# Selective-scan states written into three SBUF buffers by VectorE and multiplied by C in place, in a fused embedding, state-space and expert kernel

## The reference

```python
h = tok(x, ...)                        # (64, 128, 256): convolution and projection
h = h + attn(layernorm(h), ...)        # state-space block, below
h = h + ffn(layernorm(h), ...)         # top 2 of 8 experts, weighted sum

# attn, 512 inner channels d, 16 states n, scan over t (128 steps here; 64 sequences)
xc    = silu(causal_conv(x_inner))
delta = softplus(delta_raw * w_dt + b_dt)
h[t]  = exp(delta[t] * A) * h[t-1] + delta[t] * B[t] * xc[t]      # per d and n
y[t]  = sum_n h[t] * C[t]
out   = ((y + xc * D) * silu(z)) @ W_out
```

## Time and profile before

| | us |
|---|---|
| median of 3 runs (2647.75 to 2649.83) | 2648.08 |
| the profiled execution, its own time | 2650.71 |
| its span | 2648.9 |
| VectorE busy in the span | 2025.5 (76%) |
| GpSimd busy | 1929.2 (73%) |
| TensorE busy (modelled ends) | 2469.8 (93%) |
| ScalarE busy | 1559.3 (59%) |

### The profile page before, as it was taken

How to read it: one execution, slowest core, us unless ns; L and a number is a source line. 1 busy time by engine, 2 the same in 40 slices (tenths; PEclk the granted TensorE clock), 3 DMA queues, 4 the chain that set the end, 5 groups by cost and what they waited for, 6 DMA issues and landing times. The chain is left out here.

```text
span 2648.9 us, 35497 instructions
## 1 busy us (share of the span) xinstructions
PE 2469.8 (93%) x10678; PEld 1511.3 (57%) x10679; DVE 2025.5 (76%) x2052; ACT 1559.3 (59%) x3388; POOL 1929.2 (73%) x823
## 2 busy tenths in 40 slices
PE   4899999999999999999999999987599999999998
PEld 2334444444444444444444444433599999999998
DVE  1699999999999999999999999999333333333333
ACT  2677777777777777777777777764222222222222
POOL 2698999999999999999999999998322222222222
PEclk9999999999999999999999999999699999999999
DMA  2331414324143141431414314132532223222322
GB/s 44 141 116 43 157 39 154 116 59 158 38 154 117 58 158 38 154 120 55 158 38 154 122 53 156 39 141 88 189 47 48 46 46 48 46 47 46 47 47 33
DMA packets 124947, 235.85 MB, mean 89 GB/s; under 512 B 46031, under 2 KB 93170, under 8 KB 108460
## 3 DMA queue, kind: packets, MB, share of 16 engines
q1 hardware_dynamic: 96384, 199.06, 22.3%
q0 software_dynamic: 26272, 34.44, 7.7%
q10 hardware_dynamic: 2188, 1.15, 0.2%
HBM read 181.83 MB, written 53.65 MB: 89 GB/s over the span
## 5 line engine op out<-in xcount | busy, mean ns | idle before, releaser
L561 POOL TENSOR_TENSOR arena<-u,arena 128x2048 f32<-128x2048 f32 x255 | 1156.4, 4535 | 44.9 <-DVE psum L1180 41.2
L1180 DVE TENSOR_TENSOR_SCAN psum<-psum,arena 128x1024 f32<-128x1024 f32 x416 | 951.1, 2286 | 64.2 <-POOL arena L557 51.8
L1642 PE MATMUL psum<-hc,ident 128*128 128x512 f32 x1664 | 800.1, 605 | 95.0 <-DVE hc L1214 94.9
L891 ACT ACTIVATE psum<-delta,a_neg 128x508 f32<-128x508 f32 x1024 | 654.5, 670 | 0.0
L652 POOL DMA_INDIRECT out_dram<-hres,tok_id x135 | 210.6, 1560 | 548.1 <-ACT hres L1107 371.5
L1642 PEld LDWEIGHTS psum<-hc,ident 128*128 128x128 f32 x1664 | 298.1, 190 | 491.5 <-issue 290.7
L1214 DVE TENSOR_TENSOR hc<-psum,arena 128x1024 f32<-128x1024 f32 x416 | 507.8, 1221 | 9.9 <-PE psum L1642 0.9
L1481 DVE TENSOR_TENSOR z<-psum,xn 128x512 f32<-128x512 f32 x135 | 93.3, 691 | 432.6 <-issue 320.4
L1107 ACT ACTIVATE hres<-psum,tok_w 128x256 f32<-128x256 f32 x135 | 64.1, 475 | 400.4 <-PE psum L1817 382.6
L885 ACT ACTIVATE psum<-zeros 128x8 f32<-128x8 f32 x512 | 89.5, 175 | 303.4 <-DVE hc L1214 258.0
L1804 PE MATMUL psum<-xnt,yz 128*128 128x128 f32 x2160 | 264.9, 276 | 0.0
(11 more groups left out here) (219 smaller groups left out, 2840.5 us busy)
## 6 DMA issues: line engine op xcount, KB each, us to landing
arena<-ssm_rows SPq DMA_DIRECT2D x128, 1024.0 KB, 5.8
delta<-expert_rows SPq DMA_DIRECT2D x135, 129.0 KB, 2.0
h_saved_rows<-hnew SPq DMA_DIRECT2D x16, 512.0 KB, 6.8
hres<-h_saved_rows SPq DMA_DIRECT2D x16, 512.0 KB, 3.5
out_dram<-h SPq DMA_DIRECT2D x16, 512.0 KB, 2.9
arena<-in_L_ffn_wg_dram SPq DMA_DIRECT2D x8, 512.0 KB, 10.2
arena<-in_L_ffn_wi_dram SPq DMA_DIRECT2D x8, 512.0 KB, 10.8
arena<-in_L_ffn_wo_dram SPq DMA_DIRECT2D x8, 512.0 KB, 10.8
```

The costliest lines, as they stand in the source:

```text
L561: pool.tensor_tensor(dBx[k % 2], rep, b_rep[:, q * QN:(q + 1) * QN, :], ALU.mult).then_inc(dbx_ready, 1)
L891: last = nc.scalar.activation(o, d, ACT.Exp, scale=a_neg[:, c, n:n + 1])
L1180: nc.vector.tensor_tensor_scan(out_, h, src, 0.0, ALU.mult, ALU.add).then_inc(scan_done, 1)
L1642: last = nc.tensor.matmul(yacc[c % 2], ident[:, :], state[:, i, :], start=False, stop=(nth_sum[k] == LAST_SUM[c] and i == 1))
```

## The change

1. The scans of the 26 half units write into one of **three** buffers `hc` in SBUF; `exps` no longer finds its bank overwritten. The wait for the sum moves from the product to the scan (`sum_before`, three products back).
2. The product is taken in place in `hc`: both inputs, the state and `c_rep`, are then in SBUF.
3. As nothing overwrites dA's zero columns, they are written twice in all, at the start of group 0. `exps` waits for the scan two half units before, not for its product.
4. ScalarE's order: silu of z at k = 4 (10 before), one evacuation of `xnt` from 5 to 4 and one of `xi` from 10 to 11, the softplus pieces 2 and 3 at k = 1 and 10 (both at 4).
5. Room for the third buffer: `ones_row`, the first `pad_row`, `jlim`, `tile_no` and `tab` share the space of other tiles. Two `iota` go from the start to GpSimd's tail, `pad_row` is written again by VectorE in the tail, and in group 0 the scan k = 23 waits for the DMA that reads the first `pad_row`.

```diff
-        hc = [sb(f"hc{i}", [P, 2, GT]) for i in range(2)]
+        NHC = 3
+        hc = [sb(f"hc{i}", [P, 2, GT]) for i in range(NHC)]
...
+        def state_of(g, k):
+            return ON_POOL[k] if k in ON_POOL else flat(hc[(NOWN * g + nth_own[k]) % NHC][:, :, :])
+
+        def sum_before(g, k):
+            before, n = divmod(NOWN * g + nth_own[k] - NHC, NOWN)
+            return HU * before + nth_sum[OWN[n]] + 1
...
             def exps(g, k):
-                if k >= 2 and k - 2 in ON_POOL:
-                    actq.wait_ge(scan_done, HU * g + k - 1)
-                elif k >= 2:
-                    actq.wait_ge(hc_ready, NOWN * g + nth_own[k - 2] + 1)
-                else:
-                    ahead(actq, hc_ready, NOWN * (g - 1) + nth_own[HU + k - 2] + 1)
+                ahead(actq, scan_done, HU * g + k - 1)
                 dst = dA[k % 2]
-                nc.scalar.activation(dst.rearrange("p i (b t) -> p (i b) t", b=GB)[:, :, 0:1],
-                                     zeros[:, :].rearrange("p (b a) -> p b a", a=1), ACT.Copy)
+                if g == 0 and k < 2:
+                    nc.scalar.activation(dst.rearrange("p i (b t) -> p (i b) t", b=GB)[:, :, 0:1],
+                                         zeros[:, :].rearrange("p (b a) -> p b a", a=1), ACT.Copy)
...
-                    if k == 10:
+                    if k == 4:
                         silu_z(g)
                         if not last:
-                            evac_xi(g + 1, 1)
+                            evac_xnt(g + 1, 0)
                         load_exp_and_ln()
                     if not first:
-                        if k == 4:
-                            softplus_relu(g, 2)
-                            softplus_relu(g, 3)
+                        if k in (1, 10):
+                            softplus_relu(g, 2 if k == 1 else 3)
...
                 if k in ON_POOL:
                     state_free(g, k)
-                    out_ = ON_POOL[k]
                 else:
-                    out_ = h
-                nc.vector.tensor_tensor_scan(out_, h, src, 0.0, ALU.mult, ALU.add).then_inc(scan_done, 1)
+                    ahead(dve, sum_done, sum_before(g, k))
+                nc.vector.tensor_tensor_scan(state_of(g, k), flat(dA[k % 2]), src, 0.0, ALU.mult, ALU.add).then_inc(scan_done, 1)
...
-                if n >= 2:
-                    dve.wait_ge(sum_done, HU * g + nth_sum[OWN[n - 2]] + 1)
-                else:
-                    ahead(dve, sum_done, HU * (g - 1) + nth_sum[OWN[NOWN + n - 2]] + 1)
-                nc.vector.tensor_tensor(flat(hc[n % 2][:, :, :]), flat(dA[k % 2]), flat(c_rep[:, 2 * j:2 * j + 2, :]),
-                                        ALU.mult).then_inc(hc_ready, 1)
+                nc.vector.tensor_tensor(h, h, flat(c_rep[:, 2 * j:2 * j + 2, :]), ALU.mult).then_inc(hc_ready, 1)
```

More of the change, by code:

```diff
@@ L119, in audio_tower @@
         xt = [hres[0:KX, 2 * m:2 * m + 2, :].rearrange("p b c -> p (b c)") for m in range(2)]
+        ones_row = h2[0:1, 0, 0:P]
+        pad_first = h2[:, 2:4, :].rearrange("p b c -> p (b c)")[:, 0:ROW]
         row = sb("row", [P, GB, ROW])
@@ L148, in audio_tower @@
         ebase = sb("ebase", [P, E])
-        jlim = sb("jlim", [1, TOKENS // P])
-        tile_no = sb("tile_no", [1, NT])
+        NJL = TOKENS // P
+        jlim = draw[0:1, 0:NJL]
+        tile_no = draw[0:1, NJL:NJL + NT]
+        pad_row = draw[:, GT - ROW:GT]
+        assert NJL + NT <= GT - ROW
         cmp1 = z[0:1, 0, 0:E * (TOKENS // P)].rearrange("p (e j) -> p e j", e=E)
@@ L157, in audio_tower @@
         e_of, t_of, r_of, b_of = (hnew[0:1, i, 0:NT] for i in range(4))
-        tab = sb("tab", [1, 2, NT + 4], I32)
+        tab = xw[0:1, :, :, :].rearrange("p b k x -> p (b k x)")[:, 0:2 * (NT + 4)].bitcast(I32)\
+            .rearrange("p (k i) -> p k i", k=2)
         pad_at = sb("pad_at", [1, E], I32)
-        pad_row = sb("pad_row", [P, ROW])
         XB = 4
@@ L168, in audio_tower @@
         yt = [hres[:, i, :] for i in range(2)]
-        tok_id = [sb(f"tok_id{i}", [P, 1], U32) for i in range(XB)]
-        tok_w = [sb(f"tok_w{i}", [P, 1]) for i in range(XB)]
+        tok_ids, tok_ws = sb("tok_ids", [P, XB], U32), sb("tok_ws", [P, XB])
+        tok_id = [tok_ids[:, i:i + 1] for i in range(XB)]
+        tok_w = [tok_ws[:, i:i + 1] for i in range(XB)]
         psum = ctx.enter_context(nc.psum_tensor("psum", [P, 8, 512], F32))
@@ L187, in audio_tower @@
         LAST_SUM = [max(nth_sum[k] for k in range(HC * c, HC * c + HC)) for c in range(NCH)]
-        assert len(SUMS) == HU and NOWN % 2 == 0 and not ON_POOL.keys() & {0, 1, HU - 2, HU - 1}
+        assert len(SUMS) == HU and not ON_POOL.keys() & {0, 1, HU - 2, HU - 1}
+        def state_of(g, k):
[3 more added lines that the diff above has]
+            return HU * before + nth_sum[OWN[n]] + 1
         ssm_bank = psum[:, 7, :]
@@ L427, in _ @@
             sp.wait_ge(s_set, 1)
-            sp.dma_start(rows_dram[E * REG:E * REG + P, :], pad_row[:, :]).then_inc(padded, 16)
+            sp.dma_start(rows_dram[E * REG:E * REG + P, :], pad_first).then_inc(padded, 16)
             def step(g, par, first, second, more, last):
@@ L514, in _ @@
             pool.iota(ebase[:, :], pattern=[[REG, E]], base=0, channel_multiplier=0,
[L515 to L518, removed]
                       allow_small_or_imprecise_dtypes=True).then_inc(s_const, 1)
@@ L632, in tail @@
             def tail(g):
+                pool.iota(jlim[:, :], pattern=[[P, NJL]], base=0, channel_multiplier=0,
+                          allow_small_or_imprecise_dtypes=True).then_inc(s_const, 1)
+                pool.iota(tile_no[:, :], pattern=[[1, NT]], base=0, channel_multiplier=0,
+                          allow_small_or_imprecise_dtypes=True).then_inc(s_const, 1)
                 scatter(g - 1, 0, 0)
@@ L639, in tail @@
                 scatter_last(g)
-            pool.wait_ge(s_const, 9)
+            pool.wait_ge(s_const, 7)
             inverse_root(0, 0, stat1)
@@ L1139, in _ @@
             dve.memset(ones_e[:, :], 1.0).then_inc(s_zero, 1)
-            dve.memset(pad_row[:, :], 0.0).then_inc(s_band0, 1)
+            dve.memset(pad_first, 0.0).then_inc(s_band0, 1)
             dve.wait_ge(s_band0, 4)
-            dve.memset(pad_row[:, C:C + 1], float(TOKENS)).then_inc(s_set, 1)
+            dve.memset(pad_first[:, C:C + 1], float(TOKENS)).then_inc(s_set, 1)
             def stats_first():
@@ L1196, in state_free @@
                 if k == 23:
+                    if g == 0:
+                        dve.wait_ge(padded, 16)
                     ahead(dve, row_ready, g)
@@ L1205, in times_c @@
                     return
-                j, n = k % HC, nth_own[k]
+                j, h = k % HC, state_of(g, k)
                 dve.wait_ge(scan_done, HU * g + k + 1)
@@ L1315, in front @@
             def front():
-                dve.wait_ge(s_const, 9)
+                dve.wait_ge(s_const, 7)
                 dve.tensor_copy(counts[:, :], ebase[:, :]).then_inc(s_diag, 1)
@@ L1391, in tail @@
                 gate_y(g, NCH - 1)
+                dve.memset(pad_row[:, :], 0.0).then_inc(s_band0, 1)
+                dve.wait_ge(s_band0, 5)
+                dve.memset(pad_row[:, C:C + 1], float(TOKENS))
                 residual(g, 0, bank_a)
@@ L1420, in _ @@
             dve.wait_ge(slot_ready, G)
+            dve.wait_ge(s_const, 9)
             nc.vector.tensor_copy(pad_at[:, :], counts[0:1, :]).then_inc(pad_ready, 1)
```

13 lines of the change are left out of this document (5 added, 8 removed).

## The result

| | us |
|---|---|
| median of 4 runs (3245.63 to 3246.69) | 3246.16 |
| before, beside it, median of 4 runs (2647.54 to 2649.83) | 2647.91 |
| ratio, 95% interval | 1.2251 (1.2237 to 1.2265) |

What follows compares the result with a forecast made beforehand. VectorE was taken to bound the kernel. From 2650.7 us, 666 for products and dBx excluding each other, plus 0.5 for the tail, minus 3 for the product's own price gave 3314, predicted as 3315; range 2720 to 3610.

Steps and rivals of the forecast that it cites:

- What bounds: Group part before the change: VectorE sets the 110.1 us group, with GpSimd and TensorE within 2% of it.
- The term that decides: VectorE's two-SBUF-input products and GpSimd's SBUF-reading dBx exclude each other for whole instructions; 666 us in all, chance 0.60.
- Its size: Ten units of 9.24 us and six of 8.1, plus extras: 151.7 us a group, 41.6 more, 666 in all.
- Who wins a tie: When a unit's second scan releases product and dBx together, the product starts first, by 0.11 us.
- Zero columns: ScalarE drops 510 of 512 zero writes, 89 us, which become idle time: gain 0.
- the place of the states: VectorE's scans writing SBUF instead of PSUM: 2290 ns against 2286, cost 0.
- the sum's wait: The wait for TensorE's sum, moved before the scan, has 6.9 us of cover against 5.8: cost 0.
- The price by itself: VectorE's product with both inputs in SBUF, beside an idle GpSimd: 1213 ns against 1221, gain 3 us.
- No contention: Rival: products' second SBUF input disturbs nobody and waits for exponentials go; 2622 us, chance 0.17 (0.05 for no gain, 2648).
- The shared way: Rival: VectorE and GpSimd read SBUF at once, products are stretched; 3107 us if doubled, down to 2720; chance 0.18.
- TensorE's clock: Rival: TensorE, less busy, gets a lower clock and sets the pace; over 4200 us if throughout; chance 0.03 above the range.
- What would show it: Signs in the group part: longest product and dBx near 5.7 us, mean product 2.5 to 3.5, group about 152.

Runs made afterwards that it cites:

- second_psum: The changed kernel with the product multiplying the SBUF state by dA in PSUM instead of C, and ScalarE again released by the product: 2640.43 us.
- two_fills: The changed kernel with each dBx replaced by two zero fills on GpSimd, which only write SBUF: 2627.98 us.
- pool_writes: The changed kernel with each dBx replaced by three zero fills on GpSimd, which only write SBUF: 2876.16 us.
- psum_all: The changed kernel with scans and products back in PSUM, zero columns written again, the rest kept: 2643.37 us, ratio 0.9978 to before; repeated, 2643.24.
- split_dbx: The changed kernel with each dBx written by two GpSimd instructions of half the size: 3166.01 us.

## Why the prediction was right

*What bounds.* VectorE set the time of a group before: right. It is busy 98.6% now, but a hold counts as busy: some 39 us of a group's 147.7 (621 / 16) are its held products, and GpSimd, busy 20 us a group longer, waits in turn. Neither engine's own work fills a group any more; what bounds is that they take turns.

*The term that decides.* A full block of one engine by an instruction of the other, taken from one scaling held 3543 ns at the start of the program. Right, for this pair: second_psum and two_fills each take away one of the two readers, and each takes away the whole loss. The Trainium skill ("SBUF — State Buffer", section "Who interferes with whom") has it so, down to the remark that a GpSimd instruction that only writes doesn't collide; pool_writes agrees (median 1225 ns). The row that it was taken from bears less than I read into it, and that the whole block came out was to that extent luck. The earlier trace rows shows the longest alone; one by one, four of the 16 scalings were held, two under each of two loads. This is the third, with the load beside it:

```profile
14.41 3.29 DVE L1321 TENSOR_SCALAR diag_cw<-ident,cw 128x128 f32<-128x128 f32 x1
```

```profile
13.99 3.69 POOL L351 DMA_DIRECT2D xw<-in_x_dram  x1
```

But two scalings begun at 14.02 and 14.22, under the same load, took their usual 273 ns: that block does not span the whole instruction. Not tested is whether it has the same cause: a scaling has one input, and GpSimd was issuing loads. The row that stood against the block, a small instruction of four elements a partition, was set aside for its size. Its size didn't spare it beside a product with two inputs in SBUF: this instruction, GpSimd's inverse root, has a median of 2007 ns in the changed kernel, and lay between 1007 and 1088 before.

```profile
L540 POOL TENSOR_TENSOR rstd<-veps,half x32: 1041/2007/2039, 36.4 to 2456.7; 128x4 f32<-128x4 f32 x32
```

*Its size.* 41.6 us a group forecast, 37.6 measured; the time 3315 against 3246. The total is near, but in part because errors cancel. A unit was laid out as it stands in the rows above from the product of 1019.75 on, 1.14 + 0.1 + 4.53 + 1.14 + 2.33 = 9.24, and was to repeat. Counted from the second scan of one unit to the second scan of the next, over groups 2 to 13 (the first is 0), five of the ten units with two products take 8.9 to 9.3 us on average, four of them 0.3 less than forecast: the handoffs cost nothing (dBx ended 5.60 us after the product's start, where I had 5.77), and the held product's next scan started 1.00 after dBx ended, where I had 1.14. The other five take 10.8 to 11.7. In the group of the rows above, a GpSimd instruction had begun before the first product in each of these five, as here (the product of 1008.53 then took 5.53):

```profile
1007.95 0.66 DVE L1236 TENSOR_TENSOR h<-psum,hres 128x512 f32<-128x512 f32 x1
```

```profile
1008.47 4.50 POOL L571 TENSOR_TENSOR arena<-u,arena 128x2048 f32<-128x2048 f32 x1
```

The ten take 101.3 together. The six units with one product less, forecast at 8.1 each, take 5.6 to 10.2, 46.6 together. So where the forecast has 92.4 + 48.6 and 10.7 for GpSimd's product with C and for VectorE's small instructions, the trace has 101.3 + 46.6: 147.9 for 151.7.

*Who wins a tie.* The product, by 0.06 us in the rows above. Right for a product that follows directly on its scan. The small instructions (gate, residual, router) were put into the sum at their own length, 3.6 us a group, but they also cost the tie: of the 59 products over 5 us, 58 had one of them between the scan and themselves, and GpSimd had gone ahead. Where a product and a dBx start within 0.5 us of each other, the product is first 113 times and dBx 59 times. A product over 5 us loses 3.9 to 4.3 us (5.31 at 1029.13).

*What costs nothing.* Zero columns, the place of the states, the sum's wait, tail and shared space: right, by second_psum and psum_all.

*The price by itself.* Forecast 1213 for a mean of 1221; the median beside fills is 1225, as long as with PSUM (1224). The 3 us of gain are not there. Neither are the 65 ns a product that the Trainium skill ("VectorE: DVE Perf Modes", the section on the TRN2 errata) would give.

*The rivals.* No contention at 2622: false, but two_fills shows what it would have given, 2628. The shared way, products stretched and not blocked: false, by the rows in order of time and by split_dbx. TensorE's clock was granted at 0.91 in the group part, and the pace didn't become TensorE's: no row shows VectorE waiting for a sum before a scan. Whether the clock or the changed order made the 20 us of new waits for TensorE is not shown.

*What would show it.* Longest product 5.54 (5.7 forecast), mean 2.72 (2.5 to 3.5), a group 147.7 (about 152), dBx's longest 5.57 (5.7), the expert phase unchanged: all there.

## What to carry to other kernels

Before an operand moves from PSUM to SBUF, count the SBUF inputs of each VectorE instruction and look at what GpSimd does beside it: with two, and a GpSimd that reads SBUF most of the time, the two engines take turns, whatever the instruction's own duration says. Look also at what stands between two such instructions: a small one can decide which engine goes first. The floor is then the sum of both engines' work of that kind, and even the best order tried here stayed above it. In a profile such a hold counts as busy time of the engine that is held, so the sign to look for is not idle time but a spread of one form's durations, 1.2 to 5.5 us, where it was within 3%.

## What the runs showed of the hardware that was not expected

- The engine in waiting nearly always goes next: two products back to back let dBx in between them (6.67 us for both), so bringing such instructions together made the kernel slower (3362), until dBx was made to wait by a semaphore (3017). The exceptions are the 14 products of split_dbx that were passed by a second half.
- GpSimd's scatters, which are DMA issues and not arithmetic, are held too. Before, none of the 120 took more than 1.13 us; now 30 take over 1.3, and each of these ends 0.86 or 0.87 after a product. The reverse isn't seen: the 12 products that began during a scatter took 1.22 to 1.23 us. One scatter lasted 1.79 us in place of 0.98, beside the product that ran until 1014.06:

```profile
1008.53 5.53 DVE L1219 TENSOR_TENSOR hc<-hc,arena 128x1024 f32<-128x1024 f32 x1
```

```profile
1013.14 1.79 POOL L593 DMA_INDIRECT expert_rows<-row,slot  x1 [0.17 <-issue]
1015.23 0.98 POOL L593 DMA_INDIRECT expert_rows<-row,slot  x1 [0.30 <-issue]
```
